# Attention over graph edges: another order of VectorE, ScalarE and GpSimd work in a round, the weighting on VectorE, and a segment mask loaded from memory

## What is computed

```python
q = (x @ Wq).reshape(n, 8, 16)
wk = relu(edge_feat @ k_w1 + k_b1) @ k_w2 + k_b2          # wv likewise
k = wk * sum_s sh[:, s] * (x[edge_dst] @ Cqk[:, s, :])    # s < 9; v likewise, with Cv
attn = einsum('ehd,ehd->eh', q[edge_src], k)
amax = segment_max(attn, edge_src)                        # edge_src is the sorted index
ex = exp(attn - amax[edge_src])
den = segment_sum(ex, edge_src)
upd = segment_sum(v * ex / den, edge_src) @ W_out
```

## Time and profile before

| | us |
|---|---|
| median of 3 runs | 5793.88 (5781.95 to 5797.3) |
| profiled execution, its time | 5772.34 |
| its span | 5770.3 |
| VectorE busy | 4426.7 (77%) |
| TensorE busy | 4606.4 (80%) |
| GpSimd busy | 2985.4 (52%) |
| ScalarE busy | 2203.1 (38%) |

### The profile page before, as it was taken

How to read it: one execution, slowest core, us unless ns; L and a number is a source line. 1 busy time by engine, 2 the same in 40 slices (tenths; PEclk the granted TensorE clock), 3 DMA queues, 4 the chain that set the end, 5 groups by cost and what they waited for, 6 DMA issues and landing times. The chain is left out here.

```text
span 5770.3 us, 91299 instructions
## 1 busy us (share of the span) xinstructions
PE 4606.4 (80%) x21470; PEld 3159.0 (55%) x21470; DVE 4426.7 (77%) x9250; ACT 2203.1 (38%) x4712; POOL 2985.4 (52%) x3064
## 2 busy tenths in 40 slices
PE   2878767699999999999999999999986656565656
PEld 1222243466666666666666666666664555554545
DVE  6999843399999999999999999999973444444444
ACT  1777700155554555455555555555531000000000
POOL 1000000166666666666666666666642666565654
PEclk9999969699999999999999999999985555555555
DMA  1121235266666666666666666666631333333332
GB/s 55 78 89 67 89 129 202 67 148 147 141 140 146 146 141 142 144 145 141 140 146 145 141 143 145 143 141 143 143 74 46 81 82 81 81 83 79 81 80 58
DMA packets 530895, 665.66 MB, mean 115 GB/s; under 512 B 197864, under 2 KB 306216, under 8 KB 526888
## 3 DMA queue, kind: packets, MB, share of 16 engines
q1 hardware_dynamic: 475512, 581.31, 40.9%
q0 software_dynamic: 52288, 81.11, 6.2%
q10 hardware_dynamic: 2992, 2.09, 0.1%
HBM read 610.28 MB, written 53.94 MB: 115 GB/s over the span
## 5 line engine op out<-in xcount | busy, mean ns | idle before, releaser
L1653 POOL DMA_INDIRECT msg_rows<-a_rows,msg_idx x808 | 796.7, 986 | 620.9 <-ACT msg_idx L1625 345.7
L1505 DVE TENSOR_TENSOR attn_z<-attn_xt,attn_sh 128x512 f32<-128x512 f32 x1010 | 969.9, 976 | 27.7 <-ACT attn_xt L1226 7.1
L1285 POOL DMA_INDIRECT attn_rows<-x_twice,attn_idx x808 | 874.8, 1083 | 223.2 <-issue 205.8
L1239 ACT CAST attn_z_hi<-attn_z 128x512 fp32r<-128x512 f32 x1010 | 623.2, 620 | 617.2 <-DVE attn_z L1505 492.3
L1691 PE MATMUL msg_at_dst<-msg_bwin,msg_pick 128*128 128x64 f32 x1616 | 397.4, 428 | 547.3 <-DVE msg_pick L1717 331.0
L1303 POOL TENSOR_TENSOR acc_den<-acc_den,attn_sums 128x256 f32 x808 | 628.9, 778 | 189.2 <-POOL acc_den L1303 151.5
L1691 PEld LDWEIGHTS msg_at_dst<-msg_bwin,msg_pick 128*128 128x128 f32 x1616 | 359.9, 328 | 622.1 <-DVE msg_pick L1717 361.3
L1319 POOL TENSOR_TENSOR attn_vx<-attn_ex,attn_vw 128x512 f32<-128x512 f32 x202 | 330.7, 1637 | 587.6 <-ACT attn_ex L1264 587.6
L1511 DVE TENSOR_TENSOR attn_z_lo<-attn_z,attn_z_hi 128x512 fp32r<-128x512 f32 x808 | 554.4, 686 | 16.8
L1305 POOL MEMSET acc_den<- 128x6656 f32 x1 | 5.6, 5645 | 1057.0 <-POOLq L90 1057.0
L1631 ACT ACTIVATE msg_msg<-msg_pre 128x256 f32<-128x256 f32 x202 | 84.2, 417 | 1210.9 <-issue 617.1
(11 more groups left out here) (285 smaller groups left out, 11029.9 us busy)
## 6 DMA issues: line engine op xcount, KB each, us to landing
attn_sh<-in_edge_sh SPq DMA_DIRECT2D x404, 640.0 KB
attn_dst<-dst_scaled SPq DMA_DIRECT2D x202, 256.5 KB
attn_qwin<-q_rows SPq DMA_DIRECT2D x808, 64.0 KB
msg_dst<-dst_scaled SPq DMA_DIRECT2D x202, 256.0 KB
counts<-chunk SPq DMA_DIRECT2D x15, 3100.0 KB, 9.7
chunk_late<-counts SPq DMA_DIRECT2D x15, 3100.0 KB, 10.6
attn_feat<-in_edge_feat SPq DMA_DIRECT2D x202, 128.0 KB
msg_bwin<-b_rows SPq DMA_DIRECT2D x808, 32.0 KB
```

The costliest lines, as they stand in the source:

```text
L1239: nc.scalar.copy(z_hi[p][:, c, :], z[:, c % 2, :]).then_inc(high_sb, 1)
L1285: pool.indirect_dma_start(rows[p][:, t, :], None, dram["x_twice"], bass.IndirectOffsetOnAxis(ap=idx[p][:, t:t + 1], axis=0)).then_inc(rows ...
L1505: dve.tensor_tensor(z[:, c % 2, :], xt[p][:], sh[p][:, c, :], ALU.mult).then_inc(z_ready, 1)
L1653: pool.indirect_dma_start(rows[p][:, t, :], None, dram["a_rows"], bass.IndirectOffsetOnAxis(ap=idx[p][:, t:t + 1], axis=0)).then_inc(rows_ ...
```

## The change

The mask is loaded: set-up writes a second table `dst_step` with the scaled difference of each destination to the one before, SP loads it into `mask` behind a group's other loads, and waits for the backward scan of two groups before. `dst` loses its 513th column. VectorE does the weighting. In each engine's round the order is another, and GpSimd's additions of group g wait for the last z_lo of group g+3.

```diff
 # set-up, VectorE and SP
+            dve.tensor_tensor(line_step[:], line_prev[:], line_cur[:], ALU.subtract).then_inc(scaled_done, 1)
+            dve.wait_ge(scaled_done, 2)
+            dve.tensor_scalar(line_step[:], line_step[:], DST_SCALE, None, ALU.mult).then_inc(scaled_done, 1)
...
+            sp.dma_start(dram["dst_step"].rearrange("(p t) -> p t", p=P), line_step[:]).then_inc(scaled_out, 16)
 # GpSimd
                 pool.wait_ge(sum_sb, 2 * (g + 1))
+                pool.wait_ge(low_ready, KC * (min(g + 4, G) if isinstance(g, int) else g + 4))
...
-            with pool.Fori(1, G // 2 - 2) as n:
-                weigh(2 * n, 0)
-                gather(2 * n + 3, n + 1, 1, False)
-                make_mask(2 * n + 2, n + 1, 0, False)
-                add(2 * n - 1, 1)
...
+            with pool.Fori(0, G // 2 - 3) as n:
+                add(2 * n + 1, 1)
+                gather(2 * n + 6, n + 3, 0, False)
+                add(2 * n + 2, 0)
+                gather(2 * n + 7, n + 3, 1, False)
 # SP
-                    sp.wait_ge(masked, g - 1)
                     sp.wait_ge(pick_ready, g - 1)
-                sp.dma_start(dst[p][:], dram["dst_scaled"][bass.ds(g * GE, GE + 1)].partition_broadcast(P)
+                sp.dma_start(dst[p][:], dram["dst_scaled"][bass.ds(g * GE, GE)].partition_broadcast(P)
...
+                if not first:
+                    sp.wait_ge(topped, g - 1)
+                sp.dma_start(mask[p][:, 0:GE], dram["dst_step"][bass.ds(g * GE, GE)].partition_broadcast(P)
+                             ).then_inc(mask_in[p], 16)
 # VectorE
+            def weigh(g, p):
+
+                dve.wait_ge(ex_sb, g + 1)
+                dve.wait_ge(vw_ready, g + 1)
+                if not is_first(g, 0):
+                    dve.wait_ge(vt_ps, g)
+                dve.tensor_tensor(vx[:], ex[p][:, 0:GE], vw[p][:], ALU.mult).then_inc(vx_ready, 1)
...
-                dve.wait_ge(masked, g + 1)
+                dve.wait_ge(mask_in[p], 16 * (n + 1))
 # ScalarE
...
+                if has_two(g):
+                    take_rows(*in_two(g, n, p))
+                if back:
+                    empty_num(g - 1, q)
                 if front:
                     act.wait_ge(shifted, 2 * g + 2)
                     nc.scalar.activation(ex[p][:], ex[p][:], ACT.Exp).then_inc(ex_sb, 1)
```

More of the change, by code:

```diff
@@ L112, in setup @@
         line_scaled = ph.sb("line_scaled", [P, T])
-        before = ph.sb("before", [1, 1])
+        line_prev = ph.sb("line_prev", [P, T], I32)
+        line_step = ph.sb("line_step", [P, T])
         dst_f = ph.sb("dst_f", [P, T])
@@ L1135, in attention_loop @@
         dst_in = [ph.sem(f"dst_in{p}") for p in two]
+        mask_in = [ph.sem(f"mask_in{p}") for p in two]
         qwin_in = [ph.sem(f"qwin_in{p}") for p in two]
@@ L1158, in attention_loop @@
         sh = [ph.sb(f"sh{p}", [P, KC, GE]) for p in two]
-        dst = [ph.sb(f"dst{p}", [P, GE + 1]) for p in two]
+        dst = [ph.sb(f"dst{p}", [P, GE]) for p in two]
         qwin = [ph.sb(f"qwin{p}", [P, TG, HD]) for p in two]
@@ L1208, in is_first, with in_two, has_two @@
             return isinstance(g, int) and g == k
+        def in_two(g, n, p):
+            return g + 2, n + 1, p
+        def has_two(g):
+            return not isinstance(g, int) or g + 2 < G
         @block.scalar
@@ L1227, in prepare, with hidden @@
                 stage_idx(g + 2, p)
-                if not (is_first(g, 0) or is_first(g, 1) or is_first(g, 2)):
-                    empty(g - 3, 1 - p)
-                high(g, p, 0)
-                high(g, p, 1)
+            def hidden(g, p):
                 act.wait_ge(hid_ps, g + 1)
                 nc.scalar.activation(hid[p][:], b_hid_vt[:], ACT.Relu, bias=sb["L2_b1"][:, 0:1]).then_inc(hid_sb, 1)
-                high(g, p, 2)
             def high(g, p, c):
@@ L1243, in body @@
                 if next:
-                    prepare(*after(g, n, p))
-                else:
-                    empty(g - 2, p)
+                    high(g + 1, q, 0)
+                    high(g + 1, q, 1)
+                if not (is_first(g, 0) or is_first(g, 1)):
+                    empty_den(p)
+                if next:
+                    high(g + 1, q, 2)
+                    hidden(g + 1, q)
                 if front:
@@ L1265, in body @@
                 if is_first(g, G):
-                    empty(g - 1, q)
+                    empty_den(q)
             def first(g, n, p):
-                prepare(g, n, p)
+                take_rows(g, n, p)
+                for c in range(3):
+                    high(g, p, c)
+                hidden(g, p)
                 high(g, p, 3)
                 high(g, p, 4)
+                take_rows(*after(g, n, p))
             stage_idx(0, 0)
@@ L1491, in make_pick @@
                     dve.wait_ge(q_ps, g)
-                dve.tensor_tensor(pick[:], dst[p][:, 1:GE + 1].rearrange("p (t e) -> p t e", t=TG),
+                dve.tensor_tensor(pick[:], dst[p][:].rearrange("p (t e) -> p t e", t=TG),
                                   sb["node_of_part"][:, bass.ds(TG * g, TG)].unsqueeze(2).to_broadcast([P, TG, P]),
@@ L1519, in split_begin @@
                 make(*group, 1)
-                low(*group, 0)
-                make(*group, 2)
-                low(*group, 1)
-                make(*group, 3)
-                low(*group, 2)
-            def split_end(*group):
-                make(*group, 4)
-                low(*group, 3)
-                low(*group, 4)
+            def split_end(*group):
+                for c in range(KC - 2):
+                    low(*group, c)
+                    make(*group, c + 2)
+                low(*group, KC - 2)
+                low(*group, KC - 1)
+            def weigh(g, p):
[4 more added lines that the diff above has]
+                dve.tensor_tensor(vx[:], ex[p][:, 0:GE], vw[p][:], ALU.mult).then_inc(vx_ready, 1)
             def maxima(g, n, p):
@@ L1566, in body @@
                     dve.tensor_tensor(u[:], b_q[:], u[:], ALU.mult).then_inc(u_ready, 1)
-                if next:
-                    split_end(*after(g, n, p))
-                if front:
                     dve.wait_ge(v_ps, g + 1)
@@ L1579, in first @@
                 split_end(g, n, p)
+                make_pick(*after(g, n, p))
             dve.wait_ge(dve_set, 4)
@@ L1806, in scratch @@
             dram[name] = nc.dram_tensor(name, shape, F32, kind="Internal").ap()
[L1808 removed]
+        scratch("dst_scaled", (EP,))
+        scratch("dst_step", (EP,))
         scratch("x_twice", (NP, 2 * D))
@@ L1871 @@
         "dst_line": dst,
+        "dst_line_before": np.concatenate([dst[:1], dst[:-1]]),
         "edge_feat": np.concatenate([a["edge_attr_64"].T, np.zeros((D, pad), a["edge_attr_64"].dtype)], axis=1),
```

76 lines of the change are left out of this document (26 added, 50 removed).

## The result

The changed kernel takes **5524.75 us** (median of 4 runs, 5518.12 to 5527.73), beside 5791.9 us of the kernel before on the same chip: a ratio of 0.9539 (interval 0.9522 to 0.9556), 267 us less. The prediction was 5601 us in a range of 5568 to 5695. The direction was right, and the lock between VectorE and GpSimd went as forecast; that TensorE would then hold the loop, at 14.54 us a round, was wrong.

What follows compares the result with a forecast made beforehand. VectorE bounded the loop at 15.58 us a round; after, VectorE needs 14.3 and TensorE, the new bound, 14.54, taken as 14.6. Over 199 rounds 195 us less, 2 more for set-up: 5601 us, range 5568 to 5695.

Steps and rivals of the forecast that it cites:

- The bound before: Attention loop, 15.58 us a round: VectorE bounds it, standing behind GpSimd for 2.14 us at three places.
- VectorE after, 14.3: VectorE's need a round after the change: 12.65 + 0.60 + 0.43 + 0.10 + 0.5 = 14.3 us.
- TensorE's floor: TensorE's need a round, its waits for et and wv taken off: 14.54 us, the new bound.
- The margin to 14.6: Round taken as 14.6 us, not 14.54, for two nearly full engines and hand-overs without slack.
- (a): u behind all z_lo makes attn late: ready at 9.9 us, when VectorE reaches the forward scan; nothing lost.
- (d): ScalarE's exp behind the xt copy: w products no later, 3.3 us of ScalarE against 4.3 of TensorE.
- (b): ScalarE copies wv after the fifth cast, so TensorE's 0.50 us wait for wv goes.
- (c): ScalarE's cast ahead of vt and et is done by then, so TensorE's 0.53 us wait for et goes.
- (e) SP's queue: Mask load and the loads behind it: 1.1 us more DMA time, hidden, with cover of 2.5 us a round.
- The slower rival: sh and dst behind the mask's wait in SP's queue: 16.2 us a round, 5920 us; 6 in 100.
- (f) set-up: Outside the loop: one more load, a subtraction, a scaling and a longer store, +2 us.
- half of the lock: Additions still cost VectorE 1.2 us instead of 0.5: 15.0 a round, 5681 us; 2 in 10.

Runs made afterwards that it cites:

- b_less_pe: Kernel before with two of the four z_lo products left out of TensorE's v product: 5783.37 us, ratio 0.9997.
- a_no_gate: Changed kernel without GpSimd's wait on z_hi ahead of the additions: 5843.71 us, ratio to before 1.0074.
- the three single parts: Kernel before with only the weighting on VectorE, only the mask loaded, or only the additions held: ratios 1.0093, 1.0046, 1.0005.
- a_less_pick: Changed kernel with pick compared for one tile of four: 5222.58 us, ratio to before 0.9495.
- b_three: Kernel before, in its old order, with weighting on VectorE, mask loaded and additions held, all together: 5325.74 us, ratio 0.9681.
- a_weigh_pool: Changed kernel with the weighting back on GpSimd, behind the gathers of a round: 5705.96 us, ratio to before 0.9841.

## Why the prediction was wrong, step by step

- **The bound before (VectorE, 2.14 us of it lock)**: right. b_less_pe shows that TensorE did not count, a_no_gate that the additions did. Only the measure "each place gives its excess back" was too simple: a place gives nothing unless the work that lay there finds a better one, as the three single parts show.
- **VectorE after, 14.3**: nearly right, 14.2. The term for the additions was 0.5; measured are 0.16 at `onehot` and 0.09 at the backward scan, 0.25. Weighting at +0.43 was too low: vx is 0.65 from start to start, and the hole of 0.17 in front of the z_lo was closed by it, 0.48.
- **TensorE's floor, 15.58 - 1.04 = 14.54**: this is the step that failed. TensorE needs at most 14.12, since a_less_pick runs all of its work in that. The subtraction took for TensorE's own need what was still waiting: the 1.04 were the waits that the rows name, but a wait also costs what stands around it. Before and after, from the products of `pick` to those of the sums, and from the last v product to the transposes of vx:

```profile
2505.92 0.50 PE L1420 MATMUL attn_b_v<-attn_z_hi,L_Cv_lo 64*128 64x512 f32 x1
...
2508.54 1.05 PE L1404 MATMUL attn_b_q<-attn_pick,attn_qwin 128*128 128x128 f32 x8
2510.11 1.16 PE L1463 MATMUL attn_b_wk_sum<-attn_onehot,attn_vt 128*128 128x128 f32 x8 [0.51 <-ACT attn_et L1261]
2511.10 1.06 PE L1466 MATMUL attn_b_wv_den<-attn_onehot,attn_et 128*128 128x128 f32 x8
```
```profile
2526.09 0.50 PE L1416 MATMUL attn_b_v<-attn_z_hi,L_Cv_lo 64*128 64x512 f32 x1
2526.52 0.66 PE L1445 MATMUL attn_b_hid_vt<-ident,attn_vx 128*128 128x128 f32 x4
```
```profile
2514.16 1.05 PE L1400 MATMUL attn_b_q<-attn_pick,attn_qwin 128*128 128x128 f32 x8
2515.05 1.06 PE L1459 MATMUL attn_b_wk_sum<-attn_onehot,attn_vt 128*128 128x128 f32 x8
2515.94 1.06 PE L1462 MATMUL attn_b_wv_den<-attn_onehot,attn_et 128*128 128x128 f32 x8
```

  `pick` to sums is 1.57 before and 0.89 after: 0.68, where the row says 0.51. The first half of the sums is 0.10 longer too (0.99 against 0.89). The last v product to the transposes is 0.84 (the earlier trace rows has the later row) and 0.43: 0.41 against 0.34. The three make 1.19 in place of 0.85 in this round, and 1.36 on average between 2000 and 3000 us (0.71, 0.07 and 0.58), of the 1.44 between 15.56 and 14.12; where the rest stood is open. With 14.1 for TensorE and 14.2 for VectorE the same sum would have been 14.2 to 14.3 a round, 5521 to 5541 us.
- **The margin to 14.6** for hand-overs was 0.06 on a wrong floor. (14.6 - 14.22) x 199 = 76 us is the whole miss. By the windows view, from which the 15.58 came, the round after is 2834.66 / 199 = 14.24, and the floor accounts for 71 of the 76 us.
- **Waits (a) to (d)**: (a) was right to a tenth: "nothing to spare", 14.2; this circle is close to being a bound, though the scan waits for attn in 3 of 176 rounds only (the 0.15 above is one of them). (b) and (c) went, but not for the reason given: in b_three, with ScalarE's old order, the wait for wv is nearly gone too. So they were, at least for the most part, TensorE keeping step with a slower VectorE; that b_less_pe's wait for wv grew by just what was taken out says the same. (d) brought no wait, but the w products are where the fourth circle passes.
- **(e) SP's queue**: hidden, as forecast, with less cover. 0.80 DMA share instead of 0.70 (which was worked out on the old round; on 14.22 the same 1.1 us would give 0.77), 1.6 us of DMA time for the mask (0.80 x 14.22 - 0.63 x 15.56) instead of 1.1; one more mask, 1.9 us, already costs 0.25. The "2.5 us a round" were too many. The slower rival had the right place and didn't come to its point.
- **(f) set-up**: the first memset of the loop stands at 1123.88 instead of 1120.83 us, +3 instead of +2. Subtraction and scaling take 1.00 and 0.58.
- **The rule of the exclusive lock** (the Trainium skill, "SBUF — State Buffer", "Who interferes with whom": a VectorE instruction with two SBUF inputs contends with a GpSimd instruction that reads SBUF): the traces agree on which operations lose, z and z_lo by 0.32 and 0.44 us in a_no_gate and those with a PSUM operand by nothing. They don't bear out that it is always the second that blocks: the z of a_weigh_pool, whose row starts 0.19 us ahead of the weighting's, waits for all of it. The upper bound that I took from it, a whole addition at `onehot` and at the scan, did not come: 0.25 instead of 1.4, since the four additions of 0.64 to 0.80 lie mostly on the PSUM operations.

The rivals are all out: of "half of the lock" (1.2 us of it left, `onehot` over 1.2 or a backward scan of 1.6) there are 0.25 us, 848 ns and 1313 ns; TensorE shed its waits; the order changed something; and the loads stayed hidden.
